# A per-sequence matrix product on one Trainium2 core: eight sequences instead of four multiply W in native fp32

## What is computed

```python
attn_in = tanh(x @ W1 + b1)              # W1: 512 x 128
scores  = attn_in @ v                    # one score per row
p       = softmax(mask(type, scores))    # 128 x 128 for each sequence
x       = x + (p @ x) / cnt              # cnt: unmasked columns of the row
x       = x + x @ W[cat] + b[cat]        # W: 64 x 512 x 512, b: 64 x 512
```

## Time and profile before

| | |
|---|---|
| median of 3 runs | 312.55 us (311.0 to 312.64) |
| the profiled execution, its own time | 310.89 us |
| its span | 308.9 us |
| busy: PE, DVE, ACT, POOL | 97%, 91%, 86%, 29% of the span |
| granted TensorE clock, mean | 0.999 |
| DMA, mean over the span | 342 GB/s |

### The profile page before, as it was taken

How to read it: one execution, slowest core, us unless ns; L and a number is a source line. 1 busy time by engine, 2 the same in 40 slices (tenths; PEclk the granted TensorE clock), 3 DMA queues, 4 the chain that set the end, 5 groups by cost and what they waited for, 6 DMA issues and landing times.

```text
span 308.9 us, 4918 instructions
## 1 busy us (share of the span) xinstructions
PE 299.9 (97%) x1292; PEld 233.8 (76%) x1292; DVE 281.9 (91%) x383; ACT 266.6 (86%) x431; POOL 90.1 (29%) x123
## 2 busy tenths in 40 slices
PE   7999899899999999999999999999999999999995
PEld 4444686688787878878788887878888787888884
DVE  4459889999999999999999999999999999999961
ACT  2287988989999998999999899998989999899952
POOL 4011612334142243414224341322434132302100
PEclk9999999999999999999999999999999999999999
DMA  7999999999999999999999999999999999997243
GB/s 265 366 426 366 421 412 423 371 344 326 360 372 332 396 313 405 356 356 375 337 404 300 407 363 363 365 337 398 311 405 355 353 380 308 413 333 228 66 135 137
DMA packets 23516, 105.69 MB, mean 342 GB/s; under 512 B 2625, under 2 KB 2626, under 8 KB 13378
## 3 DMA queue, kind: packets, MB, share of 16 engines
q1 hardware_dynamic: 23202, 104.08, 90.6%
q10 hardware_dynamic: 288, 1.31, 1.1%
HBM read 88.61 MB, written 16.78 MB: 341 GB/s over the span
## 4 chain that ended last, share of the span: by engine, by line
PE 82%; DMA 6%; issue 5%; DVE 3%; ACT 1%; POOL 1%; ACTq 0%; POOLq 0%; SPq 0%; DVEq 0%
PE ps_y L653 16%; PE ps_y L655 16%; PE ps_y L654 16%; PE ps_pre L615 12%; DMA w_raw<-in_L_cond_W 6%; PE ps_y L665 4%; PE ps_y L666 4%; PE ps_y L667 4%; PE ps_y L671 3%; PE ps_pT L632 2%; PE ps_y L641 1%; PE ps_scores L625 1%; PE ps_scores L623 1%; POOL w_raw L274 1%; DVE w_lo L465 1%
## 5 line engine op out<-in xcount | busy, mean ns | idle before, releaser
L465 DVE TENSOR_TENSOR w_lo<-w_raw,w_hi 128x2048 fp32r<-128x2048 f32 x60 | 140.1, 2335 | 0.0
L336 ACT ACTIVATE w_hi<-w_raw 128x2048 fp32r<-128x2048 f32 x60 | 115.5, 1924 | 8.9 <-POOL w_raw L274 7.5
L653 PE MATMUL ps_y<-w_hi,xT_hi 128*128 128x512 f32 x240 | 95.0, 396 | 0.0
L655 PE MATMUL ps_y<-w_hi,xT_lo 128*128 128x512 f32 x240 | 93.6, 390 | 0.0
L654 PE MATMUL ps_y<-w_lo,xT_hi 128*128 128x512 f32 x240 | 93.4, 389 | 0.0
L274 POOL TENSOR_TENSOR w_raw<-w_raw,ident 128x512 f32<-128x512 f32 x30 | 39.2, 1307 | 132.6 <-DVE w_lo L465 82.6
L655 PEld LDWEIGHTS ps_y<-w_hi,xT_lo 128*128 128x128 f32 x240 | 45.0, 188 | 9.8
L654 PEld LDWEIGHTS ps_y<-w_lo,xT_hi 128*128 128x128 f32 x240 | 45.1, 188 | 9.1
L653 PEld LDWEIGHTS ps_y<-w_hi,xT_hi 128*128 128x128 f32 x240 | 45.1, 188 | 8.9 <-issue 0.2
L493 DVE TENSOR_TENSOR z_lo<-ps_y,z_hi 128x512 fp32r<-128x512 f32 x64 | 43.5, 680 | 5.4 <-ACT z_hi L372 5.3
L372 ACT ACTIVATE z_hi<-ps_y 128x512 fp32r<-128x512 f32 x64 | 38.7, 604 | 7.8 <-PE ps_y L655 5.1
(11 more groups left out here) (70 smaller groups left out, 352.8 us busy)
## 6 DMA issues: line engine op xcount, KB each, us to landing
w_raw<-in_L_cond_W SPq DMA_DIRECT2D x63, 1024.0 KB, 8.6
out<-out_sb SPq DMA_DIRECT2D x64, 256.0 KB, 6.2
x_raw<-in_x SPq DMA_DIRECT2D x15, 1024.0 KB, 7.4
out_sb<-in_L_cond_b SPq DMA_DIRECT2D x16, 256.0 KB, 5.7
x_raw<-in_x SPq DMA_DIRECT2D x2, 512.0 KB, 4.8
w_raw<-in_L_cond_W ACTq DMA_DIRECT2D x1, 1024.0 KB, 6.1
w_pack<-in_W_b_v ACTq DMA_DIRECT2D x1, 257.0 KB, 2.9
b_raw<-in_L_cond_b SPq DMA_DIRECT2D x2, 128.0 KB, 12.9
```

The lines of the kernel that those rows point to most:

```text
L336: nc.scalar.activation(w_hi[k % NH][:], w_raw[k % NW][:], ACT.Copy).then_inc(w_hi_ready, 1)
L465: nc.vector.tensor_tensor(w_lo[k % NL][:], w_raw[k % NW][:], w_hi[k % NH][:].bitcast(F32), ALU.subtract).then_inc(w_lo_ready, 1)
L653: nc.tensor.matmul(y[:], xT_hi[q][:, c, xs], w_hi[k % NH][:, c, :], start=(c == 0), stop=False)
L655: last = nc.tensor.matmul(y[:], xT_lo[q][:, c, xs], w_hi[k % NH][:, c, :], start=False, stop=(c == DC - 1))
```

## The change

`RAW` becomes 2 * G, so that all eight sequences of groups 0 and 1 take native products. `xw_raw` now takes its x from the slot of its group and waits for its PSUM bank. x of group 1 is no longer split, nor are W of sequences 4 to 7. POOL adds identities only from sequence 13 on; those of 5, 6, 9 and 10 go to DVE. W of sequence 1 is issued by ACT right behind W of sequence 0, without a wait; W of sequence 2, the next one, waits for W of sequence 0 to land (before: sequence 1's load waited for x of group 0). W of sequence 3 is loaded before that of 4, and the two halves of b before W of 4. W of sequences 9 to 12 go to slots whose last readers are now native products. The orders of ACT and DVE for sequences 3 to 8 are written anew. The diff, cut:

```diff
-    RAW = G
+    RAW = 2 * G
...
         def by_pool(k):
-            return k > G and k % G in (1, 2)
+            return k > 3 * G and k % G in (1, 2)
...
             def load_x(g):
                 if g == NX:
-                    sp.wait_ge(xw_done, RAW)
+                    sp.wait_ge(xw_done, G)
                 elif g > NX:
-                    sp.wait_ge(xT_lo_ready, g - NX)
+                    if g == NX + 1:
+                        sp.wait_ge(xw_done, RAW)
+                    else:
+                        sp.wait_ge(xT_lo_ready, x_count(g - NX))
                     sp.wait_ge(pre_done, g - NX + 1)
...
             sp.wait_ge(ids_in, 16)
-            sp.wait_ge(x0_in[1], 16)
-            load_w(1)
-            load_w(2)
+            cat_2 = load_cat(2)
+            sp.wait_ge(w_in[0], 16)
+            load_w(2, cat_2)
             load_x(1)
-            load_w(4)
             load_w(3)
-            load_w(5)
             sp.dma_start(b_raw[0:C, :], bias).then_inc(b_low_in, 16)
             sp.dma_start(b_raw[C:P, :], bias).then_inc(b_high_in, 16)
+            load_w(4)
+            load_w(5)
...
-                if b == 2 and 1 <= g < GROUPS:
+                if b == (1 if g == 1 else 2) and 1 <= g < GROUPS:
                     load_wide(g)
...
-            cat_0 = act.value_load(ids_row[0:1, 0:1], min_val=0, max_val=C - 1)
-            act.dma_start(w_raw[0][:], w[bass.ds(cat_0, 1)].rearrange("a p c h -> p (a c) h")).then_inc(w_in[0], 16)
+            for k in range(2):
+                cat = act.value_load(ids_row[0:1, k:k + 1], min_val=0, max_val=C - 1)
+                act.dma_start(w_raw[k][:], w[bass.ds(cat, 1)].rearrange("a p c h -> p (a c) h")).then_inc(w_in[k], 16)
...
             def xw_raw(k):
+                g, xs = k // G, slice((k % G) * S, (k % G + 1) * S)
+                if k >= NY:
+                    wait_out(pe, k - NY)
                 for c in range(DC):
...
-                    last = nc.tensor.matmul(ps_y[k][:], x_raw[0][:, c, k * S:(k + 1) * S], w_raw[k][:, c, :],
+                    last = nc.tensor.matmul(ps_y[k % NY][:], x_raw[g][:, c, xs], w_raw[k % NW][:, c, :],
...
             for k in range(G, B + 2):
                 g, b = k // G, k % G
-                if k < B:
+                if k < RAW:
+                    xw_raw(k)
+                elif k < B:
                     xw(k)
                 pz(k - 2)
```

More of the change, by code:

```diff
@@ L181, in wi_count, with x_count @@
         def wi_count(k):
-            return {3: 6, 4: 5}.get(k, k + 2 - pool_count(k - 1))
+            return k + 2 - pool_count(k - 1)
         def by_pool(k):
-            return k > G and k % G in (1, 2)
+            return k > 3 * G and k % G in (1, 2)
         def pool_count(k):
-            return max(k // G - 1, 0) * 2 + (min(k % G, 2) if k > G else 0)
-        assert all(pool_count(k) == sum(by_pool(i) for i in range(k + 1)) for k in range(B))
+            return sum(by_pool(i) for i in range(k + 1))
+        def x_count(g):
+            return g - RAW // G + 1
         def wide(k):
@@ L309, in _ @@
             for g in range(GROUPS):
-                if g >= 1:
-                    add_identity(G * g + 1)
-                    add_identity(G * g + 2)
+                for k in range(G * g, G * (g + 1)):
+                    if by_pool(k):
+                        add_identity(k)
                 pool.wait_ge(exp_ready, g + 1)
@@ L326, in split_xT_hi @@
                     act.wait_ge(xw_done, G * (g - NT + 1))
-                nc.scalar.activation(xT_hi[g % NT][:], x_raw[g % NX][:], ACT.Copy).then_inc(xT_hi_ready, 1)
+                nc.scalar.activation(xT_hi[g % NT][:], x_raw[g % NX][:], ACT.Copy)\
+                    .then_inc(xT_hi_ready, 1)
             def split_w_hi(k):
@@ L400, in _ @@
             nc.scalar.activation(b_both[:], b_raw[:], ACT.Copy).then_inc(b_hi_ready, 1)
-            split_w_hi(5)
+            tanh_group(1)
+            split_z_hi(3)
             split_xT_hi(2)
             exp_group(1)
-            split_z_hi(3)
             copy_out(0)
             scale_group(1)
-            split_w_hi(6)
+            split_z_hi(4)
             split_mix_hi(1)
-            split_z_hi(4)
             copy_out(2)
-            split_w_hi(7)
             split_z_hi(5)
+            copy_out(3)
+            tanh_group(2)
             split_w_hi(8)
-            tanh_group(2)
-            copy_out(3)
+            split_z_hi(6)
             split_w_hi(9)
-            for k in range(G + 3, B + 3):
+            copy_out(4)
+            exp_group(2)
+            split_w_hi(10)
+            for k in range(2 * G, B + 3):
                 g, b = k // G, k % G
@@ L545, in _ @@
             row_scale_group(0)
+            split_z_lo(1)
+            add_identity(3)
+            split_mix_lo(0)
             add_identity(4)
[L547 to L552 removed]
             dve.wait_ge(b_hi_ready, 1)
@@ L556, in _ @@
             split_z_lo(2)
+            split_av_lo(1)
+            add_identity(5)
             max_group(1)
-            split_w_lo(5)
+            split_z_lo(3)
+            add_identity(6)
             row_scale_group(1)
             split_xT_lo(2)
-            split_z_lo(3)
+            add_wide(0)
             add_identity(7)
-            add_wide(0)
-            split_w_lo(6)
+            split_z_lo(4)
             split_mix_lo(1)
-            split_z_lo(4)
             add_identity(8)
-            split_w_lo(7)
+            split_z_lo(5)
             split_av_lo(2)
-            split_z_lo(5)
+            add_identity(9)
             split_w_lo(8)
-            for k in range(G + 3, B + 1):
+            add_identity(10)
+            max_group(2)
+            split_w_lo(9)
+            row_scale_group(2)
+            split_z_lo(6)
+            add_identity(11)
+            for k in range(2 * G, B + 1):
                 g, b = k // G, k % G
```

30 lines of the change are left out of this document (12 added, 18 removed).

## The result

The changed kernel takes 313.68 us (median of 18 runs, 311.53 to 314.80), the kernel before 311.55 us beside it (18 runs, 310.48 to 312.64). The ratio is 1.0052, with a 95% interval of 1.0034 to 1.0070: 1.6 us slower by the ratio and 2.1 us between the two medians, where 0.8 us faster was forecast. The profiled execution of the changed kernel took 314.78 us, with a span of 313.0. It is one of the slower ones of a wide spread, so it shows more than the median lost.

The account below looks back on a forecast made before the run. PE bounds the kernel from 97 us, so only the stretch to about 61 us can move. 3.2 us of added PE work against 4.0 us of waits and restarts gives -0.8 us: 311.75 us, range 309.8 to 314.0.

Parts of the forecast that it names:

- the term for the loads: W of 12, issued at 51.4 us, lands at 56.3, before DVE wants it at 57.0; hidden by 0.7 us.
- The 4.9: Microseconds from issue to landing taken for W of 12, from W of 1, which had little in the queue before it.
- The first rival in the list: W of 12 lands late, holding DVE's identity of 12, `xT_lo(3)` and `hidden(3)`; at 8.2 us, 314.3 us total; chance 0.10.
- the mark: Start of `hidden(3)`, 60.93 us before, forecast at 60.1; the 0.8 us gained there is carried unchanged to the end.
- the row with 8.2 us: Issue-to-landing bound at 55.16 us, with others in front; for W of 12 it would put `hidden(3)` at 62.7 us.
- A native sequence with four products of `pz`: On PE up to `hidden(3)`: 4.43 us against 3.63, with three products 4.20 against 3.40; four sequences add 3.2 us.
- The new order of POOL: Group 1: with no identity ahead, the divisor follows the exponentials about 0.65 us sooner; transposes at 35.3 us.
- The waits at 54 to 56 us: PE's waits between 50.40 and 60.93 us vanish, including 0.80 at group 2's transposes; rival that they stay: +0.7 us, chance 0.14.
- The start: First native sequence at 9.86 us; rival that W of 0 changes: up to 0.54 us gained (0.13) or 0.3 total loss (0.10).
- both kernels do the same after `hidden(3)`: From the start of `hidden(3)` on, both kernels run alike, so the -0.8 us there stays to the end.
- each microsecond counts in full: In the late W of 12 rival (0.10), each microsecond to landing beyond 5.6 us delays `hidden(3)` by as much.

Follow-up runs that it names:

- the version that starts at 9.86 us: Changed kernel with W of sequence 1 issued by SP again and W of sequence 2 behind it: 312.97 us, ratio 1.0003 to the kernel before.
- the version that reached the mark at 59.66: Changed kernel with the identity of sequence 12 moved on DVE behind `xT_lo(3)` and `w_lo(11)`: 312.02 us, ratio 0.9993 to the kernel before.

## Why the prediction was wrong

**The step that failed** is the term for the loads: "the queue should be empty again by 51.4, so I take the 4.9: landed at 56.3, hidden by 0.7 us". It took 7.7 to 8.7 us in the changed kernel and its version with W of 1 by SP. Nor was the queue empty: in that version W of 11 was issued at 46.70 us (foreseen: 46.5) and took 5.4 us, so it landed about 0.6 us after W of 12 was issued. The 4.9 was the price of W of 1, the nearest row for an empty queue by its place, but not by its neighbours. In the new order the Ws of 12, 13 and 14, two stores and x of group 4 are let go within 4.6 us (54.02 to 58.59) once PE's product of 7 is done, right after a stretch with next to nothing in the queue. The first rival in the list described what follows from a late W of 12, and gave for 8.2 us to landing "62.7, 1.8 us later than before", which is 62.5 for 8.0 us; measured in the version that starts at 9.86 us: 8.0 us, `hidden(3)` at 62.58. So the chain was in the text with a chance of 0.10, its price at the mark was right to 0.1 us, and the row with 8.2 us stood beside the one that was chosen. The chance was wrong. Why the load takes that long here was not in the text, and that the rival's 1.8 us is near the measured loss (1.6 us by the ratio) is in part luck: the start of the changed kernel is late as well in its three profiles, and the clock fell in two of them, neither of which the rival had.

**What held.** A native sequence with four products of `pz` took 4.37 us and with three 4.12 us (4.43 and 4.20 foreseen), and in the version that starts at 9.86 us the transposes, the issue of W of 12 and PE's arrival at the mark came within about 0.1 us of the numbers given. The new order of POOL let the scaling of group 1 go sooner: 2.0 us after the start of the exponentials in that version, 2.7 before. The waits at 54 to 56 us did go (the row at 58.00 us, the transposes of group 2, has no bracket). From 97 us on nothing changed.

**What was off besides.** The start: I saw it fixed at 9.86 us, or moved by W of 1 in ACT's queue. It moves from one execution to the next, from 9.86 to 11.77 us over 17 profiles of these kernels. In the changed kernel's first profile it cost 1.25 us and W of 4 was late as well; the identity of 4 stands on DVE ahead of `av_lo(1)`, and PE waited 0.65 us for that. By the transposes of group 1 this execution was 2.5 us behind the one that starts at 9.86 us (37.81 against 35.31). The Trainium skill (DMA: Bandwidth & Descriptors, Issuing engines are not separate DMA queues) says that a second issuing engine saves issue time alone. The runs agree: ratios of 0.9979 and 0.9997 for that edit alone.

The mark was also too short a horizon. It was true that both kernels do the same after `hidden(3)`, but not that they start it alike: in the version that reached the mark at 59.66, waits of 0.67 and 0.27 us came back behind it, since DVE's loads were still late. PE earlier at the mark is worth only what DVE and the transfers can follow. And "each microsecond counts in full" was too little: after waits of 2.96 and 3.46 us the clock fell, and `hidden(3)` cost 1.4 to 1.5 us more.

**What stays open.** Why the transfers run at 209 to 385 GB/s for eight microseconds after the hole, at a share of 0.80 to 1.02, is not shown. From 52 to 60 us it is 321 GB/s on average, where the same four windows of the kernel before have 386. The version that held the later loads back puts the part of the loads behind at one to two of the three microseconds. The quarter of W of 12, issued in the same place, still took 4.7 and 4.9 us: a fourth of the bytes saved 3 to 4 us and no more. In the version with W of 12 right behind W of 10, which has no such hole, they ran at 225 to 362 GB/s between 44 and 58 us, so the hole alone is not the reason either. And whether the scatter of the start differs between the two queues can't be told from 12 and 5 profiles.

## What to carry to other kernels

When a step that used to copy an operand is taken out, the operand's buffer is held by its slower reader, and the next load into it starts later. Write down for each buffer when it comes free before and after, and when the transfers have nothing queued; in this kernel such a hole went with late loads some microseconds later, W of 12 in one version and a bias row in another. Price a load by the row with the same crowd around it, in front and behind, and where one row of the range turns the sign and the margin is under a microsecond, give it a large chance. Read the granted clock right behind each long wait of PE, and the mean clock of every run: the wait can cost more than its length.

## What was not expected of the hardware

With the same first loads in the same order, the first product that needs a whole W, which takes some 2.4 MB to have landed, starts at 9.9 us in one profile and at 11.4 us in another. After the queue had been nearly empty (53 GB/s from 48 to 50 us), a single load took 5.4 us, and the next one, issued 4.4 us later with others right behind it, 7.7 us. A wait of PE of 2.82 us left the granted clock at 1.00, and waits of 2.96 and 3.46 us before the same product were followed by a stretch at 0.50; four profiles are too few to read a rule from.
